# A skip term written into the accumulator by ScalarE instead of multiplied in by TensorE, with the engines' orders changed

## The reference, cut to what matters

```
def step(state, inp):
    h_t, d_t, g_t, B_t, C_t = inp
    dA = jnp.exp(A[None, :, :] * d_t[:, :, None])
    new = dA * state + d_t[:, :, None] * B_t[:, None, :] * h_t[:, :, None]
    y = jnp.einsum('bin,bn->bi', new, C_t) + D * h_t
    return (new, y * g_t)
```

## Time and profile before

| what | value |
| --- | --- |
| median of 3 runs | 1906.67 us (1904.21 to 1908.64) |
| the profiled execution | 1910.89 us |
| its span, first to last instruction | 1909.1 us |
| mean granted TensorE clock | 0.962 of full speed |
| PE busy | 1684.5 us, 88% of the span |
| DVE busy | 1539.7 us, 81% |
| POOL busy | 1529.5 us, 80% |
| ACT busy | 1398.8 us, 73% |

### The profile page before, as it was taken

One profiled execution on the slowest core, in us unless ns is written; L12 is line 12 of the kernel. 1 busy time (PEld: TensorE's weight loads), 2 busy tenths in 40 slices (PEclk: granted clock), 3 DMA queues, 4 the chain that ended last, 5 costly groups with the idle time before them and its releaser, 6 DMA issues. The chain is left out here.

```text
span 1909.1 us, 25699 instructions
## 1 busy us (share of the span) xinstructions
PE 1684.5 (88%) x7035; PEld 964.7 (51%) x7138; DVE 1539.7 (81%) x1891; ACT 1398.8 (73%) x4370; POOL 1529.5 (80%) x1284
## 2 busy tenths in 40 slices
PE   3679989999898999999899899989989999998976
PEld 1235454655545465554646455464645546465544
DVE  4988988888888888889888888888888888878422
ACT  5478787786977768787777869777787977867361
POOL 0578888888888888888888898888889888898734
PEclk7789999999999999999999999999999999999988
DMA  3212221313222131222213122221312222121102
GB/s 103 80 47 73 88 75 61 95 40 96 82 84 78 52 91 54 89 75 96 81 52 92 53 90 82 89 79 52 90 55 89 76 82 83 66 85 55 63 7 66
DMA packets 125918, 140.50 MB, mean 74 GB/s; under 512 B 44048, under 2 KB 69456, under 8 KB 125776
## 3 DMA queue, kind: packets, MB, share of 16 engines
q1 hardware_dynamic: 125776, 138.86, 23.8%
HBM read 133.84 MB, written 4.98 MB: 73 GB/s over the span
## 5 line engine op out<-in xcount | busy, mean ns | idle before, releaser
L1149 POOL TENSOR_TENSOR prod<-state,c_rep 128x1024 f32<-128x1024 f32 x256 | 605.4, 2368 | 39.8 <-PE p_y L627 23.7
L1018 DVE TENSOR_TENSOR_SCAN state<-decay,p_drive 128x1024 f32<-128x1024 f32 x256 | 584.6, 2284 | 28.5 <-ACT decay L766 15.2
L627 PE MATMUL p_y<-prod,ident 128*128 128x512 f32 x768 | 391.4, 609 | 10.2 <-POOL prod L1149 5.7
L766 ACT ACTIVATE decay<-delta,a_neg 128x504 f32<-128x504 f32 x512 | 359.3, 725 | 43.4 <-DVE state L1018 42.0
L1008 DVE TENSOR_TENSOR p_drive<-u,p_drive 128x1024 f32<-128x1024 f32 x256 | 312.2, 1220 | 66.4 <-PE p_drive L609 36.2
L898 ACT ACTIVATE ex<-p_ring,nmax 128x64 f32<-128x64 f32 x1024 | 310.1, 369 | 19.8 <-DVE nmax L1068 19.4
L898 ACT ACTIVATION_READ_ACCUMULATOR ex<-p_ring,nmax 128x1 f32 x1024 | 255.4, 262 | 0.0
L728 PE MATMUL p_ring<-x2T,wg 128*128 128x512 f32 x416 | 226.8, 650 | 13.2 <-ACT gh L823 12.3
L1202 POOL TENSOR_TENSOR ex<-ex,rden 128x512 f32<-128x512 f32 x128 | 144.2, 1127 | 94.1 <-DVE rden L1072 94.1
L728 PE MATMUL p_ring<-x2T,wu 128*128 128x512 f32 x416 | 208.9, 603 | 7.5 <-DVE km L1118 6.5
L627 PEld LDWEIGHTS p_y<-prod,ident 128*128 128x128 f32 x768 | 139.6, 194 | 143.8 <-issue 116.9
(11 more groups left out here) (139 smaller groups left out, 3080.1 us busy)
## 6 DMA issues: line engine op xcount, KB each, us to landing
c_rep<-c_rows SPq DMA_DIRECT2D x256, 256.0 KB, 3.6
cwr<-cw_rows SPq DMA_DIRECT2D x64, 256.0 KB, 3.2
ctxT<-in_ctx_t SPq DMA_DIRECT2D x32, 256.0 KB, 5.6
cwr<-cw_rows SPq DMA_DIRECT2D x32, 224.0 KB, 3.1
cwr<-cw_rows SPq DMA_DIRECT2D x32, 192.0 KB, 2.7
cwr<-cw_rows SPq DMA_DIRECT2D x32, 160.0 KB, 2.9
xf<-in_x SPq DMA_DIRECT2D x16, 256.0 KB, 5.9
xb<-in_x SPq DMA_DIRECT2D x16, 256.0 KB, 4.8
```

Source lines behind the costliest of these rows:

```text
L627: pe.matmul(p_y[1 - first][:], ident[:], prod[:, slot_of(c, n), 1 - first, :], start=False, stop=n == STATE - 1).then_inc(prod_used.sem, 1)
L766: act.activation(decay[:, n % 2, j, :].rearrange("p (b t) -> p b t", t=SEQ)[:, :, 1:], delta[:, c.parity, j, :].rearrange("p (b t) -> p b ...
L1018: dve.tensor_tensor_scan(state[:, slot_of(c, n), :, :].rearrange("p j t -> p (j t)"), decay[:, n % 2, :, :].rearrange("p j t -> p (j t)"), ...
L1149: pool.tensor_tensor(mine, state[:, slot_of(c, n), :, :], c_rep[:, n % C_SLOTS, :].unsqueeze(1).to_broadcast([128, HALVES, T]), ALU.mult). ...
```

## The change: what it does

ScalarE now does `y_d`: one ACTIVATE of `h` with the scale D (one value for each partition), written straight into the PSUM bank `p_y[j]`. The sums no longer begin with `start=True`: the first `y_sum` of each bank waits for ScalarE's write and adds to it. Two matmuls before the first turn write each bank once, so that later matmuls without a start add to what is there. The diagonal matrices are no longer made.

```diff
-            def skip_d(c, i):
-                j = 1 - i
-                pe.wait_ge(h_ready.sem, h_ready.at(c.m, j))
-                if c.m >= 1:
-                    pe.wait_ge(yg_ready.sem, yg_ready.at(c.m - 1, i))
-                pe.matmul(p_y[j][:], diag_d[:, j, :], h[:, c.parity, j, :], start=True, stop=False)
+            for j in range(HALVES):
+                pe.matmul(p_y[j][:], ident[:], wattn[:].rearrange("d w o -> d (w o)"),
+                          start=True, stop=True).then_inc(y_open.sem, 1)
             def sum_n(c, k):
                 n, first = divmod(k, HALVES)
+                if sum_index(k) < HALVES:
+                    pe.wait_ge(skip_ready.sem, skip_ready.at(c.m, first))
...
                 pe.matmul(p_y[1 - first][:], ident[:], prod[:, slot_of(c, n), 1 - first, :],
-                          start=False, stop=n == STATE - 1).then_inc(prod_used.sem, 1)
+                          start=False, stop=n == STATE - 1, skip_group_check=True
+                          ).then_inc(prod_used.sem, 1)
...
+                elif name == "y_d":
+                    j = 1 - i
+                    act.wait_ge(h_ready.sem, h_ready.at(c.m, j))
+                    if c.m >= 1:
+                        act.wait_ge(yg_ready.sem, yg_ready.at(c.m - 1, i))
+                    else:
+                        act.wait_ge(y_open.sem, y_open.at(0, j))
+                    act.activation(p_y[j][:], h[:, par, j, :], ACT.Copy, scale=column(V_D + j)
+                                   ).then_inc(skip_ready.sem, 1)
...
-            for j in range(HALVES):
-                dve.tensor_scalar(diag_d[:, j, :], ident[:], column(V_D + j), None,
-                                  ALU.mult).then_inc(consts_v.sem, 1)
```

All the tables of the order are new as well, on every engine and in all three parts. Two lines of the ScalarE list for the turns between, as a sample:

```diff
-        "front.hid1 front.gate0 back.k0 scan.decay5 front.tap1 back.norm0 back.v0 scan.decay6 "
+        "front.tap1 back.k0 scan.y_d0 scan.y_d1 front.gate0 scan.decay5 scan.decay6 back.v0 "
```

More of the change, by code:

```diff
@@ L76 @@
     "pe": (
[16 rows of a table removed]
-    "act": (
[15 rows of a table removed]
-    "dve": (
[12 rows of a table removed]
-    "pool": (
[7 rows of a table removed]
+        "back.v0 back.mout0 back.mout1 back.x1T0 front.gate0 back.v1 scan.B_row3 back.x1T1 back.q0 "
+        "scan.B_row4 back.score0 back.score1 scan.B_row5 back.score2 scan.y_sum2 scan.y_sum3 "
+        "back.score3 back.turn0 scan.y_sum4 scan.y_sum5 scan.y_sum6 back.turn1 scan.B_row6 "
+        "scan.y_sum7 back.mix0 tail.down0 back.turn2 back.score4 back.mix1 scan.B_row7 scan.y_sum8 "
+        "back.mix2 scan.y_sum9 back.turn3 back.score5 scan.B_row8 back.mix3 front.xp0 back.turn4 "
+        "back.score6 scan.B_row9 front.less0 scan.y_sum10 scan.y_sum11 front.less1 scan.y_sum12 "
+        "back.score7 back.turn5 back.aout0 scan.B_row10 scan.y_sum13 tail.down1 back.mix4 "
+        "scan.y_sum14 back.turn6 back.mix5 scan.y_sum15 scan.B_row11 back.turn7 back.mix6 front.dt0 "
+        "back.mix7 scan.B_row12 back.aout1 front.dt1 scan.y_sum18 back.x2T0 scan.y_sum19 back.x2T1 "
+        "scan.B_row13 back.route0 back.up_g0 back.up_g1 back.up_u0 back.up_u1 scan.y_sum22 "
+        "scan.B_row14 scan.y_sum23 back.up_g2 back.cwT0 back.up_u2 front.gate1 back.up_g3 back.up_u3 "
+        "back.up_g4 back.up_g5 scan.y_sum26 scan.B_row15 scan.y_sum27 back.up_u4 back.up_u5 "
+        "back.up_g6 back.up_g7 back.up_u6 back.up_g8 front.B_row0 back.up_u7 head.xnT0 back.up_u8 "
+        "head.xnT1 back.up_g9 back.up_g10 back.up_u9 back.up_g11 scan.y_sum28 scan.y_sum29 "
+        "front.B_row1 back.up_u10 head.hid0 head.hid1 scan.y_sum30 back.up_u11 scan.y_sum31 "
+        "back.up_g12 back.up_u12 scan.k0 front.B_row2"),
+    "act": (
[16 rows of a table added]
+    "dve": (
[12 rows of a table added]
+    "pool": (
[7 rows of a table added]
     "sp": (
[4 rows of a table removed]
[4 rows of a table added]
 }
@@ L376, in build @@
         bqs = sb("bqs", [128, 2])
-        diag_d = sb("diag_d", [128, HALVES, 128])
         mhalf = sb("mhalf", [128, GROUPS])
@@ L463, in build @@
         ready_const = signal("ready_const")
-        bv_ready = signal("bv_ready")
+        bv_ready, y_open = signal("bv_ready"), signal("y_open", HALVES)
         consts_v = signal("consts_v")
-        CONSTS = 10
+        CONSTS = 8
         ring_full = [signal(f"ring_full{i}") for i in range(BANKS)]
@@ L490, in build @@
         prod_used = signal("prod_used", SUMS)
+        skip_ready = signal("skip_ready", HALVES)
         yg_ready = signal("yg_ready", 2)
@@ L636, in step @@
                     spread_b(c, i)
-                elif name == "y_d":
-                    skip_d(c, i)
                 elif name == "y_sum":
```

## The result

The changed kernel took 1966.78 us (median of 4 runs, 1960.13 to 1975.45) against 1907.66 us for the one before in the same comparison: a ratio of 1.031, with 95% between 1.0285 and 1.0336. So it is slower by 3%, where I had forecast 1888.5 us, a ratio of 0.990. The profiled execution took 1975.45 us (span 1973.6); its mean granted clock was 0.935, before 0.962.

What follows compares the result with a forecast made beforehand. Attention was taken as led by the ScalarE-VectorE softmax chain, the rest by TensorE with GpSimd close behind. Gains of 0.4 + 0.6 + 0.3 = 1.3 us over 14 turns, 18.2 us, gave 1888.5 us against the median; range 1867 to 1915.

Steps and rivals of the forecast that it cites:

- what comes: ScalarE's two ACTIVATEs, TensorE's opening matmuls and SyncE's reordered C loads: covered or 0, opening matmuls at worst 0.3 us.
- y_d off TensorE: Attention, behind q: the 1.72 us a chunk filled TensorE's wait for qs, so taking them out gives 0.
- Rival D: Less TensorE work in attention makes the clock fall right after it: 12 us of gain go, 1900.5 us; 8%.
- y_d on ScalarE: Behind the copy of k: 1.3 us a chunk, covered by ScalarE's 4.55 us wait before the first norm.
- The new orders: First score 0.4, experts 0.6 and first norm 0.3: 1.3 us gained a chunk, 18.2 us over 14 dense turns.
- the 1.15 us for the gate's copy: Experts: TensorE's wait for a bank mostly goes; gain 0.6 us a chunk, bounds 0 and 1.15.
- The 0.3 for the first norm: GpSimd's norm ahead of last cw: down stalls 0.7 us, x1T's 1.02 us wait goes; net gain 0.3 a chunk.
- the late first score: Attention: exp 0 about 1.1 us later, absorbed by ScalarE's 1.29 us wait; exp 5 comes 0.4 us earlier.
- rival C: Attention: the late first maximum isn't swallowed, exp 5 is 1.1 us late each chunk; slower, 1922 us; 22%.
- A: TensorE leads throughout, so the 1.72 us count as well: 3.0 us a chunk, 1864.5 us; 15%.
- B: Nothing is left: GpSimd's cw chain makes TensorE wait at down, gains paid back; 1906.7 us within 3; 14%.
- The list of signs: Profile after: attention over 50.5 us shows rival C, under 48.9 A; second stretch 60.1 B; clock 0.97 in every chunk Rival D.

Runs made afterwards that it cites:

- e1: The changed kernel with SyncE's loads of xb, ctx and x ahead of the C9 load again: 1892.55 us, ratio 0.9909.
- e4: The kernel before, its orders kept, with only y_d moved from TensorE to ScalarE behind the copy of k: 1925.20 us, ratio 1.0076.
- e6: e1 with y_d back on TensorE behind q, as in the code before the change: 1891.72 us, ratio 0.9909.
- e9: The changed kernel with SyncE's C7, then xb, ctx and x loads ahead of C9, and GpSimd's last cw ahead of the norm again: 1888.23 us, 0.9891.
- e10: The changed kernel, SyncE's C7, xb, ctx, x ahead of C9; first score ahead of B_row 5, first maximum ahead of state 5's multiplication: 1881.45 us, 0.9859.
- e5: e4 plus two useless 128x512 matmuls on TensorE ahead of the first score, in that score's bank: 1908.42 us, ratio 1.0003.
- e3: The kernel before with SyncE's C9 ahead of the xb, ctx and x loads and C8 ahead of the output store: 1929.48 us, ratio 1.0107.
- e8: The changed kernel with only the load of x moved behind C7 in SyncE's list: 1955.73 us, ratio 1.0253.

## Why the prediction was wrong, step by step

**The step that failed** is the last sentence on what comes: "SyncE's list is cut elsewhere and reorders its C loads; C has four slots, and in rows 10 GpSimd waits for the `cw` rows, not for C: 0." Its price is 6.2 us a full turn, 74 us in all (after against e1). The reasoning had two holes. Rows 10 show the last `cw` and the norm, another place in the turn than the one where the list was changed. And four slots say how early a row may be asked for, not how early it is: `C7` had a free slot and stood behind `C9`, which had none, and, new with the change, behind four loads. The range, up to 1915 us, held no term for it, so the time fell outside.

How the 74 us come about: a wait of 6.06 us on GpSimd, of which 4.20 reach TensorE at `turn` 5, and after it matmuls at the low clock, in the rest of attention (0.90) and in the first expert matmuls (0.72). In e1 `turn` 5 waits for nothing, the clock shows no fall in the rest of attention (table above), and is 0.86 behind it. Its `turn` 5, and the window behind attention:

```profile
948.58 0.65 PE L695 MATMUL p_ring<-ident,ex 128*128 128x128 f32 x4
```

```profile
964.10:976.50 12.40, 11.86 (x34) 5.84 (x35) 11.07 (x20) 8.72 (x17) 9.01 (x7) 0.86 0.16 46
```

From `q`, `turn` 5 starts after 32.99 us in e1 and after 37.30 in after, 4.3 us late. The other 1.9 of 6.2 us a turn come behind it. How much of the whole is the clock can be estimated. The same 7078 matmuls are busy 1692.6 us in after and 1661.7 in e1:

```profile
PE 1661.7 (88%) x7078; PEld 953.1 (50%) x7078; DVE 1518.9 (80%) x1889; ACT 1425.7 (75%) x4402; POOL 1549.2 (82%) x1284
```

That is 31 us of longer instructions, and by the table 77 us more at half speed cost at most 38. So some 30 to 40 of the 74 us are matmuls at the low clock and the rest are waits. This is an estimate from two profiles; no run took the clock alone away in this kernel.

**y_d off TensorE: 0.** In e4 the wait grew from 0.46 to 2.17 us, as forecast, and the term is 0 in the new orders (e6 and e1 both 0.9909). In the old ones it is not 0 but a loss of 0.8% (e4), by the clock. Rival D had the mechanism, with 12 us and after attention; it sat at the scores instead, in twelve of thirteen full turns, and cost 15 us there (e4 against before).

**y_d on ScalarE: 1.3 us a chunk, covered.** 1.36 us of work, 1.30 as a pair, behind `k` where ScalarE waits. Nothing waits for it. The Trainium skill (page ScalarE: Activation LUTs, section Step-by-step: what each stage is for) had PSUM as the faster place to write to; 0.68 us against the 0.807 to SBUF in the earlier trace rows agrees, though the two read different tiles as well, and no run changes the target alone.

**The new orders: 1.3 us a turn.** Right in sum: 111.9 less 110.6 is 1.3 from before to e1, and 0.9909 stands beside the 0.9905 forecast. Less so in its parts, so that the sum came out so close is partly luck. In the turn of e1 shown above attention gained 1.2 us, not 0.4 (50.10 to 48.90), and the rest did not reach 59.2 but 60.50, between the 60.10 and 61.40 of the earlier trace rows. Over eleven middle turns, cut at `q` and at the second transpose of x2, attention gained 0.8 us (49.45 to 48.67) and the rest 0.6 (62.44 to 61.83), where the forecast had 0.4 and 0.9. Of the waits, the 1.15 us for the gate's copy and ScalarE's 1.29 us before `exp` 5 are gone in e1, and the 1.02 us of `x1T` have become 0.59 at `q`. The wait of 0.7 us for the last `cw` inside `down` doesn't show in the full turns. The 0.3 for the first norm can't be measured, though (e9). And the late first score did cost: e10 takes some 7 us back by undoing it, 0.5 us a turn. That is rival C at half its price, paid inside a gain.

**The rivals.** A, with TensorE leading throughout, is out: 1.72 us less on it gave nothing. B is out by e1. C and D were each right in kind and small. D had read two chunks as a fall of the clock behind attention in every other turn; before the change it falls there in nine of thirteen full turns. In the new orders it is low for longer there, 59 us in e1 and 48 in e6, which has `y_d` on TensorE, against 35, so more by the orders than by `y_d`. The loss of 3% was in none of the rivals. The list of signs even pointed at the wrong one: "if attention is over 50.5 us, C holds" was met by 54.27 us, which came from SyncE and not from the late first maximum. All of that list looked at the four computing engines.

## What to carry to other kernels

When an order of DMA issues changes, follow each entry through: what the entry ahead of it waits for, how long the loads between take to issue, when its consumer is due; that a buffer is free says nothing as long as the entry that would fill it stands behind one that waits. And price an operation that is taken from TensorE ahead of a wait not only by its own time but by the clock behind it: in e4 and e5 two useless matmuls ahead of a wait gave back 14 to 17 us over the run. Before a change of this kind is judged as a whole, its one cheap part (here one list) is worth running alone, since 74 us of loss hid 17 us of gain.

## What the runs showed of the hardware

- Issuing a 256 KB load took SyncE 0.3 to 0.6 us, but what came fifth in a close row took far longer: 2.90 us for `xf` in after, 2.86 us in before, 2.58 in e3, and 3.23 us for two C rows in e8, in which `xf` then went in 0.44 us. Without a C row right ahead of them (e1), `xf` as the fourth took 1.18 us. What fills up there, no row shows.
- An ACTIVATE with a scale of 128x512 float32 from SBUF to PSUM took 0.682 us; the nearest from PSUM to SBUF in the earlier trace rows is 0.590, from SBUF to SBUF 0.807.
- The two scores behind a wait of 2.17 us took 3.43 us, and behind one of 0.35 us, filled with useless matmuls, 1.98 us. The granted clock from 2 to 8 us behind `q` was 0.68 to 0.77 in twelve of thirteen full turns of the first (e4), and 1.00 in all of the second (e5).
